# Other byte offsets for the standing operands of TensorE in a fused attention and channel-mix block

## The reference

```python
xn = _layernorm(x)                                   # x: (8, 1024, 256)
# attention: 8 heads of 128, one shared key and value head
q = (xn @ Wq + bq).reshape(B, T, 8, 128) + pe
k, v = split(xn @ Wkv + bkv);  k = k + pe
probs = softmax(causal(q @ k.T / sqrt(128)))
attn = (probs @ v).reshape(B, T, 1024) @ Wo
# channel mix
xr = mu_r * xn + (1 - mu_r) * xn_prev                # xn_prev: shifted by one token
xk = mu_k * xn + (1 - mu_k) * xn_prev
ffn = sigmoid(xr @ W_r.T) * (square(relu(xk @ W_k.T)) @ W_v.T)
return x + attn + ffn
```

## The kernel before, in words

| work | standing | moving | columns | matmuls |
|---|---|---|---|---|
| scores (S) | `qt` | `kt` | 16 to 512 | 2304 |
| query projection (Q) | `wq` | `xt` | 256 | 1536 |
| key and value projection (KV) | `wkv` | `xt` | 256 | 384 |
| channel mix, key (FK) | `wk` | `mh` | 256 | 384 |
| channel mix, gate (FR) | `mh` | `wr` | 256 | 384 |
| channel mix, value (FV) | `kh` | `wv` | 256 | 384 |
| output projection (WO) | `ot` | `wo` | 256 | 1536 |
| probabilities x values (PV) | `v`, `vn`, `vs` | `pt` | 256 | 3344 |
| transposes | `X`, `xn`, `kv`, `ident` | `ident` | 128 | 1468 |

## Time and profile before

### The profile page before, as it was taken

One profiled execution on the slowest core, in us unless ns is written; L12 is line 12 of the kernel. 1 busy time (PEld: TensorE's weight loads), 2 busy tenths in 40 slices (PEclk: granted clock), 3 DMA queues, 4 the chain that ended last, 5 costly groups with the idle time before them and its releaser, 6 DMA issues.

```text
span 1504.9 us, 36254 instructions
## 1 busy us (share of the span) xinstructions
PE 1482.6 (99%) x11724; PEld 1448.2 (96%) x11724; DVE 1268.4 (84%) x3424; ACT 1068.0 (71%) x2563; POOL 1128.9 (75%) x1541
## 2 busy tenths in 40 slices
PE   7999999999999999999999999999999999999998
PEld 7999999999999999999999999999999999999998
DVE  6999878898788987998879888798977888789885
ACT  6777667776677767767677776776767777677764
POOL 6687777777777877777777776777777787777875
PEclk8999999999999999999999999999999999999999
DMA  4144422444224442244423444134441344403453
GB/s 129 48 131 129 142 75 64 134 125 147 72 65 133 135 134 68 83 120 137 134 60 88 127 128 144 46 98 128 134 141 34 113 131 138 136 27 108 119 157 105
DMA packets 225801, 164.39 MB, mean 109 GB/s; under 512 B 51792, under 2 KB 220880, under 8 KB 225616
## 3 DMA queue, kind: packets, MB, share of 16 engines
q1 hardware_dynamic: 224768, 161.69, 35.6%
q10 hardware_dynamic: 848, 0.40, 0.1%
HBM read 81.27 MB, written 77.59 MB: 106 GB/s over the span
## 4 chain that ended last, share of the span: by engine, by line
PE 81%; DVE 10%; issue 4%; POOL 3%; DMA 1%; ACT 1%; SPq 0%; DVEq 0%; POOLq 0%; ACTq 0%
PE pS L1040 27%; PE pO L1181 22%; PE pG L1040 13%; PE pG L1127 9%; PE pT L1143 8%; DVE X L1019 2%; DVE pt L943 1%; DVE Y L923 1%; DVE kt L831 1%; POOL X L571 1%; DVE xn L808 1%; DMA park_dram<-Y 1%; DVE mix L860 1%; POOL qt L527 1%; DVE qtmp L849 1%
## 5 line engine op out<-in xcount | busy, mean ns | idle before, releaser
L764 ACT ACTIVATE X<-X,bias 128x16 f32<-128x16 f32 (+56 forms) x512 | 376.1, 734 | 150.7 <-DVE bias L1019 149.0
L1040 PE MATMUL pS<-kt,qt 128*128 128x288 f32 (+41 forms) x2304 | 460.1, 329 | 4.5 <-DVE bias L1019 3.4
L571 POOL TENSOR_SCALAR X<-X,rec 128x16 f32<-128x16 f32 (+56 forms) x512 | 378.2, 739 | 44.2 <-DVE rec L913 33.4
L1040 PEld LDWEIGHTS pS<-kt,qt 128*128 128x128 f32 x2304 | 365.7, 189 | 17.1 <-issue 5.3
L546 POOL TENSOR_TENSOR pt<-pt 128x256 fp32r<-128x256 f32 (+5 forms) x192 | 316.6, 1649 | 60.3 <-ACT pt L686 59.8
L1181 PE MATMUL pO<-pt,v 128*128 128x256 f32 x2192 | 307.6, 284 | 1.2 <-DVE ot L998 0.9
L1019 DVE CUSTOM_DVE_ANT_1 X<-pS,mask 128x528 f32<-128x528 f32 (+31 forms) x256 | 245.6, 959 | 47.1 <-PE pS L1040 42.3
L1181 PEld LDWEIGHTS pO<-pt,v 128*128 128x128 f32 x2192 | 271.9, 189 | 2.6 <-DVE ot L998 2.1
L943 DVE TENSOR_TENSOR pt<-pt,pT 128x512 fp32r<-128x512 f32 (+3 forms) x440 | 207.6, 493 | 35.1 <-ACT pt L692 32.2
L757 ACT CAST ot<-pO 128x256 fp32r<-128x256 f32 x256 | 95.5, 373 | 184.0 <-PE pO L1181 117.8
L692 ACT CAST pt<-pT 128x512 fp32r<-128x512 f32 (+3 forms) x448 | 188.0, 450 | 30.8 <-PE pT L1143 30.5
(11 more groups left out here) (120 smaller groups left out, 2298.6 us busy)
## 6 DMA issues: line engine op xcount, KB each, us to landing
park_dram<-Y SPq DMA_DIRECT2D x32, 512.0 KB, 2.6
pt<-park_dram SPq DMA_DIRECT2D x128, 128.0 KB, 2.8
park_dram<-Y SPq DMA_DIRECT2D x32, 448.0 KB, 3.0
pt<-park_dram SPq DMA_DIRECT2D x128, 112.0 KB, 2.5
park_dram<-Y SPq DMA_DIRECT2D x32, 384.0 KB, 2.9
pt<-park_dram SPq DMA_DIRECT2D x128, 96.0 KB, 2.3
park_dram<-Y SPq DMA_DIRECT2D x32, 320.0 KB, 2.7
pt<-park_dram SPq DMA_DIRECT2D x128, 80.0 KB, 2.1
```

The lines of the kernel that those rows point to most:

```text
L571: nc.gpsimd.tensor_scalar(x_row(s, 0, w), x_row(s, 0, w), rec[:, j:j + 1], sign(s), ALU.mult, ALU.mult).then_inc(normed, 1)
L764: nc.scalar.activation(x_row(s, 0, w), x_row(s, 0, w), ACT.Exp, bias=bias[:, j:j + 1], scale=-1.0, accum_out=total[:, j:j + 1]).then_inc(e ...
L1040: last = nc.tensor.matmul(out, a[i], m[j], start=start and k == 0, stop=stop and k == n - 1)
```

## The change

Only the placement of tiles in SBUF changes; no instruction is added, removed or reordered. `gap` shrinks from 64 to 32 bytes, three more unused tiles of 32 bytes are put in (`gap3`, `gap4`, `gap5`), tiles are declared in another order, and `kh` and `ot` become views that start 16 bytes into a larger tile. By sizes this gives, in bytes beyond a multiple of 128:

| tile | role | before | after |
|---|---|---|---|
| `wk`, `wkv` | stand | 64 | 32 |
| `v`, `vs`, `vn` | stand | 64 | 64 |
| `wr` | moves | 64 | 64 |
| `wq`, `qt` | stand | 64 | 96 |
| `kh` | stands | 64 | 112 |
| `ot` | stands | 64 | 16 |
| `mh` | moves (FK), stands (FR) | 0 | 0 |
| `xt`, `wv`, `kt`, `pt`, `wo` | move | 0 | 0 |

`gap5` brings `bq` back to 64; everything from `bq` on lies 128 bytes further than before and keeps its place beyond a multiple of 128.

```diff
-        gap = sb("gap", [P, 16])
-        wq = [sb(f"wq{i}", [P, CT, H * D], R) for i in range(2)]
+        gap = sb("gap", [P, 8])
         wk = [sb(f"wk{i}", [P, CT, E], R) for i in range(2)]
         wkv = [sb(f"wkv{i}", [P, CT, 2 * D], R) for i in range(2)]
-        wr = [sb(f"wr{i}", [P, CT, E], R) for i in range(2)]
-        kh = [sb(f"kh{i}", [P, CT, CHUNK], R) for i in range(2)]
-        qt = [sb(f"qt{i}", [P, 2, CHUNK // SUB, H, SUB], R) for i in range(2)]
+        gap3 = sb("gap3", [P, 8])
         v = [sb(f"v{i}", [P, NT, D], R) for i in range(2)]
         vs = sb("vs", [P, TPC, D], R)
         vn = sb("vn", [P, NT, D], R)
-        ot = [sb(f"ot{i}", [P, H, P], R) for i in range(2)]
+        wr = [sb(f"wr{i}", [P, CT, E], R) for i in range(2)]
+        gap4 = sb("gap4", [P, 8])
+        wq = [sb(f"wq{i}", [P, CT, H * D], R) for i in range(2)]
+        qt = [sb(f"qt{i}", [P, 2, CHUNK // SUB, H, SUB], R) for i in range(2)]
+        kh_both = sb("kh", [P, 2 * CT * CHUNK + 8], R)
+        kh = [kh_both[:, 4 + i * CT * CHUNK:4 + (i + 1) * CT * CHUNK].rearrange("p (t n) -> p t n", t=CT)
+              for i in range(2)]
+        ot_both = sb("ot", [P, 2 * H * P + 8], R)
+        ot = [ot_both[:, 4 + i * H * P:4 + (i + 1) * H * P].rearrange("p (h q) -> p h q", h=H) for i in range(2)]
+        gap5 = sb("gap5", [P, 8])
         bq = sb("bq", [P, H])
```

## The result

The changed kernel takes 1514.8 us (median of 3, 1512.02 to 1515.44) against 1504.0 us. The ratio is 1.0070, with a 95% interval of 1.0047 to 1.0094: slower, where faster was forecast, and just above the range of 1486 to 1513. The profiled execution took 1512.02 us with a span of 1510.3 us, and it was the fastest of the three.

A forecast was written before the change was run, and what follows sets the result against it. PE's own stream was taken as the bound. Slow kinds -6.6, fast kinds +1.9 and scores 0 gave -4.7 us; 0.85 of it, -4.0 us, took the median from 1504.0 to 1500.0 us, range 1486 to 1513.

The forecast's parts named there:

- The bound: Whole kernel: PE's own stream, busy 99% of the span, sets the time; 0.85 of its change reaches the end.
- The weight load itself: PE's weight loads from the moved standing tiles: no change in duration, bounded at 5 ns either way.
- Kinds at the slow level: `ot`, `wq` into pG, `wk` into pS (2652 matmuls, median 281 ns): slow half turns 5 ns faster, -6.6 us.
- Kinds at the fast level: `wq` into pS, `kh`, `wk` into pG, `wkv` (1548 matmuls): can lose up to +7.7 us; a quarter taken, +1.9 us.
- Scores: The 2304 score matmuls with `qt` standing: taken as 0, with 11.5 us possible in either direction.
- The moving stream beside a load: A matmul's read beside a load's read: their distance modulo 128 may count; wide scores suggested 0 to -12 ns per matmul.
- Other engines: ScalarE, VectorE and GpSimd writing moved tiles: any longer writes hidden, taken as 0; without cover +10 us for `ot`.
- Place does not decide: Rival on PE's matmul pace: what ran just before sets the two levels; time 1504 within 3 us; chance 0.32.
- the rule cited ahead: TensorE's independent read ports for moving operand and weight loads: no distance between them could matter, time stays at 1504.
- The scores get slower: Rival at L1213: load of `qt` at 96 meets `kt`'s stream worse, +11.5 us; time 1511.5, or 1519; chance 0.25.
- A much better meeting: Rival: moved 256-column matmuls reach the transposes' 109 ns spacing, -30 us, -45 or more with scores; 1460 to 1475; chance 0.05.
- The range: Predicted time of the whole kernel, 1486 to 1513 us, held for 8 in 10.

## Why the prediction was wrong, point by point

**The bound** held. PE's stream set the time in every kernel, and 0.85 was a fair share to let through: 10.8 of 12.9 us here by the medians (5.4 by the two profiled spans), and 0.79 to 1.06 in the kernels tried.

**The weight load itself** held nearly: 1 to 2 ns instead of none, inside the bound of 5. Weight loads after, count, busy us, mean ns:

```profile
L1133 PEld LDWEIGHTS pG<-wo,ot 128*128 128x128 f32 x1536 | 187.9, 190 | 1.5 <-ACT ka L745 0.8 <-issue 0.7
...
L1046 PEld LDWEIGHTS pG<-wv,kh 128*128 128x128 f32 x192 | 23.9, 189 | 0.0
```

They take 190 ns for `ot` at 16 and 189 for `kh` at 112, where it was 189 for `ot` in the same view of before and 188 for `kh`. With all standing tiles at 0 it was 191 for `ot` and 190 for `kh`. A longer load does not explain the spacing: with all at 128, the load of `ot` took 188 ns and its spacing was 118.8.

**Kinds at the slow level** is the step that failed. It put -6.6 us on the slow half of `ot`, `wq` and `wk` turning fast. Measured on the same matmuls, it was +7.4 us: `wo,ot` +3.6 ns x 1536, `wq` into pG +1.6 ns x 924, `wk` into pS +1.9 ns x 192. I had read the two levels as a toss that a new place would throw again, with more to win where more was slow. But at 144, where `ot` went, none of its 64 groups is fast, and the fast level was seen at 64 and 192 alone (the table above). Of the distances at which all kinds were put (0, 32, 48, 64, 80, 128, 192), 64 is the one with an average under 117 ns; 96, 112 and 144, which single kinds had, gave 118.0 to 119.7. A mixture at one place said that this place had access to both levels. It did not say that another would have it.

**Kinds at the fast level** had the right sign and was too small. I put +1.9 us of a possible +7.7, with the slow level of 118 ns as the worst; the same matmuls lost 6.3 us (`wq` into pS +4.0 ns x 600, `kh` +5.4 x 384, `wk` into pG +4.3 x 192, `wkv` +2.7 x 372). `kh` went from 114.1 to 119.5 ns, beyond the slow level, and `ot` to 119.7; I had named a pace outside 113 to 118 ns as something that would make the prediction wrong altogether. There is more than one step.

**Scores** at 0 held: 460.4 us against 460.1, and 1.0003 when `qt` moved alone.

**The moving stream beside a load** pointed to the right cause and was read from the wrong kind. I took the scores' widths as the nearby case and found an offset worth 0 to -12 ns. But the scores turned out to be the one kind whose pace does not follow the distance, and so a few ns among their widths said nothing for the others. They even pointed the other way: the second halves at 496 and 488 columns have distances 0 and 32 from `qt` and came out faster than the line, and 0 and 32 are bad for the kinds of 256 columns. A nearer row stood in the same trace: `wr,mh` was the one kind at another distance (192 modulo 256), and its durations in the trace of before, shortest/median/longest, were

```profile
L1040 PE MATMUL pG<-wr,mh x192: 277/279/363, 104.0 to 1462.9; 128*128 128x256 f32 x192
```

Its spacing was 117.8 ns, the slowest of the kinds whose moving slice is one run, where those at 64 had 114.1 to 116.1. In the kernels where it stayed at 192 it was between 115.7 and 117.8 ns, so this row is a hint and no more, but it was a hint against a place other than 64.

**Other engines** held, as far as the end is concerned. Groups by shape after, on the moved tiles:

```profile
L1187 PE MATMUL pO<-pt,v 128*128 128x256 f32 x2192 | 308.5, 285 | 1.1 <-DVE ot L1004 0.9
L1187 PEld LDWEIGHTS pO<-pt,v 128*128 128x128 f32 x2192 | 273.3, 189 | 2.3 <-DVE ot L1004 2.0
L1133 PE MATMUL pG<-wo,ot 128*128 128x256 f32 x1536 | 199.5, 287 | 0.9 <-ACT ot L763 0.6 <-ACT ka L745 0.2
...
L533 POOL TENSOR_TENSOR qt<-qtmp,qt 128x512 fp32r<-128x512 f32 x124 | 164.1, 1326 | 62.0 <-ACT qt L665 61.9
...
L1004 DVE TENSOR_TENSOR ot<-pO,ot 128x256 fp32r<-128x256 f32 x256 | 107.2, 419 | 57.1 <-ACT ot L763 52.7
...
L763 ACT CAST ot<-pO 128x256 fp32r<-128x256 f32 x256 | 95.7, 374 | 195.1 <-PE pO L1187 121.7 <-PE pO L1196 62.6 <-PE pG L1133 9.4
```

`ot` takes 374 and 419 ns (373 and 418 before), `qt` 1326 (1310); PE still waits only 1.1 us for `qt`, once.

**The rivals.** "Place does not decide" is refuted by +1.42% at distance 0 with the same instructions, and with it what I had concluded from the rule cited ahead. The Trainium skill, "SBUF — State Buffer", section "Who interferes with whom", has TensorE's two reads on independent ports and PE waiting on no one; by that, the two streams could not disturb each other. The measurement decides: the pace of loads and matmuls depends on the distance between what they read, by 3.9 ns in 115 over all kinds and by 5.4 for `kh`. Whether it is the ports or something behind them isn't shown. "The scores get slower" gave the time, 1511.5 to 1519, by luck: its mechanism did not happen. The sign came from the fast kinds and the supposed winners. "A much better meeting" did not appear at any distance.

**The range** ended at 1513 because I held that not every kind would go the same way. All five moved kinds of 256 columns did, since all left the same good distance. The sum by kinds in the prediction's own terms was +7.4 + 6.3 = +13.7 us where it had -6.6 + 1.9 = -4.7.

## What to carry to other kernels

When a placement in SBUF is in question on a PE-bound kernel, compute for each kind of matmul the distance between what the load and the matmul beside it read, modulo 256, and compare kinds at different distances in the trace that you have. Read the spacing, not the median duration. Here 64 was the best, 16 bytes off lost half of it or more, and moving both operands by 32 bytes together did nothing. And when one place shows both a fast and a slow level, the place may already be the good one: ask what share of it is fast, and what other places show, before counting the slow share as a gain to be had.

## What the runs showed of the hardware

- A matmul of 256 float32r columns follows the one before it after 113 to 114 ns in a fast group, and after up to 120 ns on average of a kind, at the full clock (granted 0.996 to 0.999 in every run, the level of 2.4 GHz), with the same instructions. Groups hold a level: the 24-groups of before average 113.5 to 114.3 ns or 117.7 to 117.8 ns, none between. The fast one occurs at distance 64 (27 to 51 of 64 groups) and 192 (7 and 18), and at none of 0, 32, 48, 80, 128, 144.
- The pace depends on the difference of the two addresses, with a period of 256 bytes as far as was tried: 64 and 320 alike (115.5 and 115.1 ns), 192 worse (117.1), and 0, 32, 48, 80 and 128 worse still (118.2 to 119.4). This is for a moving slice in one run.
- Scores, whose widths run from 16 to 512 columns, do not follow it: 459.5 us at distance 0, 460.1 at 64, 460.4 in the changed kernel (spacing 168.2, 168.6 and 168.5 ns). Why is open. That their second halves start at changing distances is no full answer, as the first halves always start at the same one. Whether it is their width, or what they read, was not tried.
- What in the memory makes the distance matter was not shown. That it lies between the two reads, and not in either alone, follows from the runs with both shifted (by 32 bytes, +0.06%) and with only one shifted. The loads of the larger kinds take 188 to 192 ns on average in every kernel, the longest with distance 0, and do not follow the spacing (188 ns for `ot` at 128, spacing 118.8).
